# Two strips' exponents by one matmul of twelve rows, and the mask added second and only on the diagonal blocks

## The chip, the cores and the metric

The kernel runs on one core of one Trainium2 chip. The time is the device time of one execution in microseconds. The kernel before took 896.44 us (median of three runs, 891.09 to 898.82). TensorE is the matmul engine (PE in the profile, its weight loads PEld), VectorE is DVE, ScalarE is ACT, GpSimd is POOL, SyncE is SP and issues the DMAs here.

## What is computed

The input is x of 32 sequences, 256 tokens, 128 features, in f32. Four layers follow one another, each `x = x + layer(layernorm(x))`: a gated delta-rule attention, a feed-forward layer, a state-space layer, the same feed-forward layer. The change is in the state-space layer only:

```
zxbcdt = h @ W_in                                 # z 256, xBC 512, dt 4 columns
xBC = silu(causal_conv(xBC, 4 taps)); x, B, C = split(xBC)   # 4 heads of 64; state 128
dt = softplus(dt + dt_bias);  A = -exp(A_log)
# state-space scan over the whole sequence, per head:
#   y[i] = sum over j <= i of  (C[i].B[j]) * exp(S[i] - S[j]) * dt[j] * x[j]
#   S = running sum of dt*A
y = (y + x * D) * silu(z)
y = y * rsqrt(mean(y*y) + eps) * norm_w;  out = y @ W_out
```

The reference writes the scan in chunks of 32 with a carried state; the kernel computes the same as one masked product over all 256 tokens of a sequence. For that it needs, per sequence and head, a matrix of exp(S[i] - S[j]) for j <= i and zero elsewhere. With the source token j on 128 partitions it is cut in two strips: source tokens 0 to 127 against all 256 targets, and source tokens 128 to 255 against targets 128 to 255, 256 + 128 = 384 columns (the name TRI).

## The kernel before, in words

A group is four tiles of 128 tokens, which is two sequences (called batches in the code). There are 16 groups. The state-space part is a software pipeline of 18 halves, `space_half`: half h convolves and projects group b = h, makes exponents, products and scores of group e = h - 1, and outputs of group f = h - 2; up to half 9 it also normalises and transposes the x of a later group (x, turn), and projects dt of a later group (d). Each engine has its own instruction stream, written out by hand in this order, with semaphores between them; there is no planner. TensorE's order in a half is `space_half` from L1779: gate projection L1738, exponents of head 0 of sequence 1 (`log_decay(e, 0, 1)`), head outputs L1761 of group f in two parts with a convolution L1734 between them, transposes L1769 and L1476, exponents (0, 0), L1734, dt projection L1718 (d), exponents (1, 1), products of B and C L1775, exponents (1, 0) and (2, 1) in a row, the sum of squares L1832, gate projection L1738, exponents (2, 0), L1769, L1734, exponents (3, 1) and (3, 0) in a row, the output projection L1853, L1734.

The exponents S[i] - S[j] are themselves made on TensorE, by `log_decay`, in f16 with f32 accumulation. S is split into three f16 pieces (`split_sums`, PIECES = 3; the last is scaled and weighted by TINY). For each group of a quad (four groups, j of them at partitions 32 j) six partitions hold, in turn, piece rows and constant rows: `from_rows` has the pieces of S on even partitions and the weights on odd ones, `to_rows` the negative weights on even and the pieces on odd. A product of the two over the six rows gives S[i] - S[j]. The mask `never16` has -30000 where the target lies before the source (in the two diagonal 128 x 128 blocks) and zero in the block between. One exponent group in `log_decay` is three matmuls into one PSUM bank: the mask times an f16 identity over all 384 columns (L1747), six rows over 256 columns for the first strip (L1748), six rows over 128 columns for the second (L1750). Then ScalarE takes the exponential of the 384 columns (L897), GpSimd multiplies by the products of C and B (L644), and L1761 multiplies by x. A half has eight groups, and there are 16 halves with them: 128 groups.

The pieces reach `from_rows` and `to_rows` through DRAM. Once per quad, SyncE writes `pieces` to `pieces_dram` (L511), waits for it, and issues for each of the quad's four groups two DMAs, one into `from_rows` (L517) and one into `to_rows` (L518), each of three runs of 4096 bytes. There are two sides of the rows, for even and odd quads. The constants of each side are first filled by GpSimd in `set_rows` (L637, two casts of 2048 columns a side): side 0 in the preparation before the first half, side 1 behind half 0. VectorE makes `ident16` and `never16` once (L1213 to L1216). TensorE waits for a group's rows by `pieces_in` at L1784.

VectorE adds an output to x in `add_residual` (L1224), and L1761 of the next half waits for that. ScalarE normalises (L741), makes the first tap (L876); VectorE makes the other three (L1352).

Of the kernel before, what the change touches and what calls it, by code (L numbers as in the profile page):

```python
# [5 lines left out]
BATCH, SEQ, DIM = 32, 256, 128  # L6
# [6 lines left out]
P = 128  # L13
TILES = BATCH * SEQ // P
GROUP_TILES = 4
# [16 lines left out]
PIECES = 3  # L32
TINY = 2.0 ** -12
# [17 lines left out]
def constants():  # L51
# [21 lines left out]
def build(nc, x_in, Wq, bq, Wk, bk, Wv, bv, Wa, ba, Wb, bb, Wg, bg, Wo, bo,  # L73
# [7 lines left out]
    with ctx:  # L81
# [19 lines left out]
        tab = sb("tab", [P, (4 + len(LEVELS)) * P + 2 + LEAF * LEAF])  # L101
# [5 lines left out]
        from_side, to_side = (tab[:, after_keep + P + k:after_keep + P + k + 1] for k in range(2))  # L107
        two_eye = tab[0:GROUP_TILES * LEAVES, after_keep + P + 2:]
# [100 lines left out]
        from_rows, to_rows = ([flat_ff[u][:, k * 2 * GROUP:(k + 1) * 2 * GROUP].bitcast(f16) for u in U] for k in range(2))  # L209
# [4 lines left out]
        ident16, never16 = sb("ident16", [P, P], f16), sb("never16", [P, TRI], f16)  # L214
# [209 lines left out]
        def _(sp):  # L424
# [80 lines left out]
            for q in range(GROUPS // QUAD):  # L505
                side = q % 2
                sp.wait_ge(split_step, SPLITS * (q + 1))
                if q >= 2:
                    for j in range(QUAD):
                        sp.wait_ge(pieces_in[side][j], 16 * 2 * (q // 2))  # L510
                sp.dma_start(pieces_dram[side].rearrange("m r c -> r m c"), pieces[:, :, :]).then_inc(pieces_out, 16)  # L511
                sp.wait_ge(pieces_out, 16 * (q + 1))
                sp.wait_ge(rows_set, 2 * min(q + 1, 2))
# [16 lines left out]
        def _(pool):  # L530
# [438 lines left out]
        def _(dve):  # L969
# [244 lines left out]
            for strip_at in (0, SEQ):  # L1214
                nc.vector.tensor_copy(never16[:, strip_at:strip_at + P], never).then_inc(prep_done, 1)
            nc.vector.tensor_copy(never16[:, P:SEQ], eye_zero[:, P:2 * P]).then_inc(prep_done, 1)  # L1216
# [695 lines left out]
```

## Time and profile before

| | |
|---|---|
| median of three runs | 896.44 us |
| the three runs | 896.44, 891.09, 898.82 us |
| the profiled execution | 890.48 us |
| its span, first to last instruction | 888.6 us |
| PE busy | 783.3 us (88%) |
| DVE busy | 627.1 us (71%) |
| POOL busy | 562.5 us (63%) |
| ACT busy | 537.4 us (60%) |
| mean granted TensorE clock | 0.944 of full |

The span is that of the same execution as the 890.48. The first feed-forward layer starts at about 352 us (the attention before it) and ends at about 436 us, the preparation of the state-space part lies between 436 and 485 us, its first exponent group at 485.5 us, its last at 777.5 us, and the second feed-forward layer starts at about 798 us. A row of a timeline joins instructions of one line that follow one another. A matmul's recorded duration reaches on past the start of the next matmul, so durations of neighbours overlap.

### The profile page before, as it was taken

What the parts mean: (1) busy time and instruction counts of PE and PEld (TensorE: products, weight loads), DVE (VectorE), ACT (ScalarE), POOL (GpSimd) and SP (SyncE); (2) the same over time, 40 slices, a digit from 0 to 9 for tenths busy, and PEclk for the clock granted to TensorE, in tenths of its full rate; (3) what the DMA queues carried; (4) which work ended last, traced back from release to release, by engine and by line L of the source; (5) the groups of instructions that cost most, each with busy time, mean ns of one, the idle gap of its engine ahead of it and who ended that gap; (6) DMA issues with size and microseconds to landing.
All of it is one profiled execution on the core that took longest, in us unless ns stands there. A gap on an engine that the chain in (4) does not pass through costs nothing. (4 is left out here: it accounts for less than half of the span.)

```text
span 888.6 us, 16307 instructions
## 1 busy us (share of the span) xinstructions
PE 783.3 (88%) x5274; PEld 557.7 (63%) x5274; DVE 627.1 (71%) x1740; ACT 537.4 (60%) x1036; POOL 562.5 (63%) x899
## 2 busy tenths in 40 slices
PE   1379999999999895999748999999999999959997
PEld 1268888888888773666534456555555555546665
DVE  1356778777778643888665868988787776537885
ACT  2224443344344324989645878888888787728885
POOL 0266566666766611887632488769778866757785
PEclk9859999999999899999956999999999999979999
DMA  7411211111121100000000000000000000000112
GB/s 215 110 27 31 51 28 28 41 42 27 28 54 28 28 14 1 1 1 0 2 0 7 0 2 7 3 1 1 8 1 1 8 1 1 1 0 25 47 48 72
DMA packets 57740, 22.07 MB, mean 25 GB/s; under 512 B 20960, under 2 KB 57312, under 8 KB 57664
## 3 DMA queue, kind: packets, MB, share of 16 engines
q1 hardware_dynamic: 57664, 21.13, 9.2%
q8 instruction: 38, 0.62, 0.3%
q14 instruction: 38, 0.31, 0.1%
HBM read 11.49 MB, written 9.63 MB: 24 GB/s over the span
## 5 line engine op out<-in xcount | busy, mean ns | idle before, releaser
L1352 DVE SCALAR_TENSOR_TENSOR arena<-bank,convw_sb,arena 128x510 f32<-128x510 f32 (+2 forms) x192 | 142.6, 745 | 37.3 <-ACT arena L876 32.5
L644 POOL TENSOR_TENSOR arena<-arena 128x768 f32<-128x768 f32 x64 | 115.0, 1817 | 12.9 <-ACT arena L903 12.9
L621 POOL TENSOR_TENSOR arena<-ff,arena 128x512 f16<-128x512 f32 x64 | 73.7, 1161 | 23.1 <-ACT arena L844 21.0
L556 POOL TENSOR_TENSOR leaf_tmp<-leafV 32x14 f32<-32x14 f32 (+6 forms) x224 | 56.2, 251 | 33.0 <-DMA leafV<-LT_dram 17.8
L741 ACT ACTIVATE xn<-x_all,shift,rstd 128x128 f32<-128x128 f32 x136 | 55.6, 480 | 33.3 <-DVE shift L988 33.2
L1734 PE MATMUL bank<-xnT,win_sb 128*128 128x512 f32 x128 | 72.5, 651 | 3.2 <-DVE arena L1352 3.2
L839 ACT ACTIVATE ff<-bank 128x512 f32<-128x512 f32 x96 | 56.3, 586 | 30.9 <-PE bank L1645 30.7
L540 POOL TENSOR_TENSOR var_eps<-mv,eps_cols 128x4 f32<-128x4 f32 x34 | 7.6, 223 | 105.0 <-DVE mv L981 86.5
L748 ACT ACTIVATE ff<-bank 128x256 f32<-128x256 f32 (+2 forms) x80 | 34.0, 425 | 66.0 <-PE bank L1489 37.5
L560 POOL TENSOR_TENSOR leafV<-leafV,leaf_tmp 32x14 f32<-32x14 f32 (+6 forms) x224 | 62.6, 279 | 17.5
L897 ACT ACTIVATE arena<-bank 128x384 f32<-128x384 f32 x128 | 60.1, 491 | 21.9 <-PE bank L1750 21.7
L1178 DVE SCALAR_TENSOR_TENSOR ff<-bank,ff 128x512 f32<-128x512 f32 x96 | 64.7, 684 | 10.0 <-ACT ff L839 9.4
L733 ACT ACTIVATE xnT<-bank 128x512 f32<-128x512 f32 x34 | 20.2, 596 | 77.8 <-PE bank L1476 77.8
L650 POOL TENSOR_TENSOR arena<-arena 128x512 f32<-128x512 f32 x32 | 40.3, 1272 | 38.2 <-DVE arena L1359 37.9
L1015 DVE SCALAR_TENSOR_TENSOR arena<-bank,arena 128x256 f32<-128x256 f32 (+1 forms) x128 | 44.6, 411 | 25.0 <-PE bank L1561 16.0
L876 ACT ACTIVATE arena<-bank,convb_sb,convw_sb 128x512 f32<-128x512 f32 x64 | 49.9, 779 | 12.0 <-PE bank L1734 12.0
L1761 PE MATMUL bank<-arena 128*64 128x256 f32 (+1 forms) x512 | 48.5, 332 | 1.7 <-DVE x_all L1224 1.2
L1476 PE MATMUL bank<-tab,xn 128*128 128x128 f32 x136 | 24.6, 311 | 27.8 <-issue 16.5
L1761 PEld LDWEIGHTS bank<-arena 128*64 128x64 f32 x512 | 31.8, 136 | 24.3 <-issue 13.7
L1644 PE MATMUL bank<-xh,gate 128*128 128x512 f16 x96 | 37.7, 393 | 8.6 <-DVE xl L1163 7.9
L1747 PE MATMUL bank<-never,ident 128*128 128x384 f16 x128 | 42.4, 331 | 0.6 <-ACT arena L897 0.6
L844 ACT ACTIVATE arena<-ff 128x512 f16<-128x512 f32 x64 | 39.8, 622 | 3.4 <-DVE ff L1178 3.4
(202 smaller groups left out, 2260.6 us busy)
## 6 DMA issues: line engine op xcount, KB each, us to landing
LT_dram<-arena SPq DMA_DIRECT2D x16, 256.0 KB, 2.4
ff<-R_dram SPq DMA_DIRECT2D x16, 256.0 KB, 2.9
out<-x_all SPq DMA_DIRECT2D x8, 512.0 KB, 3.2
x_all<-in_L_attn_a_x SPq DMA_DIRECT2D x7, 512.0 KB, 7.0
tab<-in_tables SPq DMA_DIRECT2D x1, 513.0 KB, 5.2
x_all<-in_L_attn_a_x SPq DMA_DIRECT2D x2, 256.0 KB, 3.1
R_dram<-tab SPq DMA_DIRECT2D x2, 256.0 KB, 2.7
leafV<-LT_dram SPq DMA_DIRECT2D x16, 32.0 KB, 2.6
```

The lines of the kernel that those rows point to most:

```text
L556: nc.gpsimd.tensor_tensor(prod, V[:, s:s + 1, s + 1:LEAF].broadcast_to([leaf_rows, s, below]), V[:, 0:s, s:s + 1].broadcast_to([leaf_rows, ...
L560: nc.gpsimd.tensor_tensor(V[:, 0:s, s + 1:LEAF], V[:, 0:s, s + 1:LEAF], prod, ALU.subtract).then_inc(leaf_step, 1)
L621: nc.gpsimd.tensor_tensor(of_block(hl[u], j), hidT[u][:, j, :], of_block(hh[u], j), ALU.subtract).then_inc(hl_done[u], 1)
L644: nc.gpsimd.tensor_tensor(score[h], cb[g % 2], hgam[h], ALU.mult).then_inc(score_done, 1)
L741: last = nc.scalar.activation(xn[u][:, cols(t)], x_all[:, n % GROUPS * GROUP + t * P:n % GROUPS * GROUP + (t + 1) * P], ACT.Identity, scal ...
L839: nc.scalar.activation(silu_g[u][:, j, :], bank[u][(1, 3, 1)[j]][:, :], ACT.Silu, scale=DEQUANT).then_inc(silu_done[u], 1)
L876: nc.scalar.activation(xbc[r][b % 2], conv_bank[r % 2][:, :], ACT.Identity, scale=convw_sb[:, r, TAPS - 1:TAPS], bias=convb_sb[:, r:r + 1] ...
L897: nc.scalar.activation(hgam[h][:, batch * TRI:(batch + 1) * TRI], step_bank[batch][:, 0:TRI], ACT.Exp).then_inc(hgam_done, 1)
L1178: nc.vector.scalar_tensor_tensor(hidT[u][:, j, :], bank[u][(2, 0, 2)[j]][:, :], DEQUANT, silu_g[u][:, j, :], ALU.mult, ALU.mult).then_inc( ...
L1352: nc.vector.scalar_tensor_tensor(acc_of[:, :, s:SEQ], src_of[:, :, 0:SEQ - s], convw_sb[:, r, TAPS - 1 - s:TAPS - s], acc_of[:, :, s:SEQ], ...
L1734: mm(conv_bank[r % 2][:, :], win_sb[:, INNER + r * P:INNER + (r + 1) * P], xnT[b % XNT_SETS][:, :], start=True, stop=True).then_inc(conv_m ...
L1761: last = mm(y_bank[r][k * HEAD_DIM:(k + 1) * HEAD_DIM, batch * SEQ + c * P:(batch + 1) * SEQ], x_of[:, 2 * batch + c, h * HEAD_DIM:(h + 1) ...
```

## The change

`log_decay` has two matmuls instead of three. The first has twelve rows: six for each strip. Both strips' pieces stand on twelve partitions of `from_rows`, which now has 128 columns for a head instead of 256: the first strip's source tokens on rows 0 to 5, the second's on rows 6 to 11. `to_rows` has 384 columns for a head instead of 256; a strip's six rows are zero in the other strip's columns. One matmul of 384 columns then gives both strips and opens the accumulation. The second matmul adds the mask, times the identity, and only in columns 0 to 127 and 256 to 383 of the bank; `never16` has 256 columns instead of 384.

Each of the quad's DMAs is cut in two, one a strip, with runs of 256 or 512 bytes, so four for a group (PIECE_DMAS) instead of two. `set_rows` has three copies instead of two for a side, of 1024, 2048 and 1024 columns. The tables have one more column. VectorE makes `never16` with two casts instead of three.

```diff
-    piece, side = (r % 32) // 2, r % 2
-    weight = np.where(piece < PIECES - 1, 1.0, np.where(piece == PIECES - 1, TINY, 0.0))
+    of_strip, side = (r % 32) // 2, r % 2
+    strip_at, piece = of_strip // PIECES, of_strip % PIECES
+    weight = np.where(strip_at > 1, 0.0, np.where(piece < PIECES - 1, 1.0, TINY))
     parts.append((weight * (side == 1)).astype(np.float32))
-    parts.append((-weight * (side == 0)).astype(np.float32))
+    for k in range(2):
+        parts.append((-weight * (side == 0) * (strip_at == k)).astype(np.float32))
...
                 for j in range(QUAD):
-                    src = pieces_dram[side][:, j * BATCHES * HEADS:(j + 1) * BATCHES * HEADS, :].rearrange("m r c -> m (r c)")
-                    sp.dma_start(from_rows[side][32 * j:32 * j + 2 * PIECES:2, :], src).then_inc(pieces_in[side][j], 16)
-                    sp.dma_start(to_rows[side][32 * j + 1:32 * j + 1 + 2 * PIECES:2, :], src).then_inc(pieces_in[side][j], 16)
+                    src = pieces_dram[side][:, j * BATCHES * HEADS:(j + 1) * BATCHES * HEADS, :]
+                    of_quad = slice(32 * j, 32 * (j + 1))
+                    for k in range(2):
+                        at = 2 * PIECES * k
+                        froms = from_rows[side][of_quad, :].rearrange("p (r c) -> p r c", c=P)[at:at + 2 * PIECES:2]
+                        tos = to_rows[side][of_quad, :].rearrange("p (r c) -> p r c", c=TRI)[at + 1:at + 1 + 2 * PIECES:2, :, k * SEQ:k * P + SEQ]
+                        sp.dma_start(froms, src[:, :, k * P:(k + 1) * P]).then_inc(pieces_in[side][j], 16)
+                        sp.dma_start(tos, src[:, :, k * P:SEQ]).then_inc(pieces_in[side][j], 16)
...
             def set_rows(side):
-                for dst, weight in ((from_rows[side], from_side), (to_rows[side], to_side)):
-                    nc.gpsimd.tensor_copy(dst, weight.broadcast_to([P, 4 * GROUP])).then_inc(rows_set, 1)
+                nc.gpsimd.tensor_copy(from_rows[side], from_side.broadcast_to([P, 2 * GROUP])).then_inc(rows_set, 1)
+                of_head = to_rows[side].rearrange("p (r c) -> p r c", c=TRI)
+                for k, strip_cols in enumerate((slice(0, SEQ), slice(SEQ, TRI))):
+                    nc.gpsimd.tensor_copy(of_head[:, :, strip_cols],
+                                          to_side[k].unsqueeze(1).broadcast_to([P, BATCHES * HEADS, SEQ - k * P])).then_inc(rows_set, 1)
...
-                rows = slice(32 * j, 32 * j + 2 * PIECES)
+                rows = slice(32 * j, 32 * j + 4 * PIECES)
                 to = step_bank[batch]
-                a = (batch * HEADS + h) * SEQ
+                at = batch * HEADS + h
                 pe.wait_ge(hgam_done, past(decay_at(e, h, batch) - BATCHES))
-                mm(to[:, 0:TRI], ident16[:, :], never16[:, :], start=True, stop=False)
-                mm(to[:, 0:SEQ], from_rows[side][rows, a:a + P], to_rows[side][rows, a:a + SEQ],
-                   start=False, stop=False)
-                mm(to[:, SEQ:TRI], from_rows[side][rows, a + P:a + SEQ], to_rows[side][rows, a + P:a + SEQ],
-                   start=False, stop=True).then_inc(E_mm, 1)
+                mm(to[:, 0:TRI], from_rows[side][rows, at * P:(at + 1) * P], to_rows[side][rows, at * TRI:(at + 1) * TRI],
+                   start=True, stop=False)
+                mm(to[:, 0:TRI].rearrange("p (s c) -> p s c", c=P)[:, 0:3:2, :], ident16[:, :],
+                   never16[:, :].rearrange("p (s c) -> p s c", c=P), start=False, stop=True).then_inc(E_mm, 1)
```

## Rows read from the trace of the kernel before

**Rows 1.** The page, part 1: busy time of each engine, its share of the span, instructions.
```profile
PE 783.3 (88%) x5274; PEld 557.7 (63%) x5274; DVE 627.1 (71%) x1740; ACT 537.4 (60%) x1036; POOL 562.5 (63%) x899
```

**Rows 2.** Sums by window: stretch, length, each engine's busy time (instructions), clock, DMA.
```profile
500.00:520.00 20.00, 18.66 (x103) 10.71 (x103) 15.45 (x38) 15.27 (x28) 12.24 (x10) 0.91 0.00 1
540.00:560.00 20.00, 20.00 (x127) 12.21 (x127) 15.77 (x36) 16.96 (x32) 17.85 (x18) 1.00 0.03 9
```

**Rows 3.** TensorE's timeline, 561 to 582 us: start, duration, instruction, tiles, form, count.
```profile
561.35 1.02 PE L1734 MATMUL bank<-xnT,win_sb 128*128 128x512 f32 x2
562.22 1.02 PE L1738 MATMUL bank<-xnT,win_sb 128*128 128x512 f32 x2
563.07 0.33 PE L1747 MATMUL bank<-never,ident 128*128 128x384 f16 x1
563.33 0.28 PE L1748 MATMUL bank<-ff 6*128 6x256 f16 x1
563.45 0.21 PE L1750 MATMUL bank<-ff 6*128 6x128 f16 x1
563.60 1.52 PE L1761 MATMUL bank<-arena 128*64 128x256 f32 x16
565.05 1.12 PE L1734 MATMUL bank<-xnT,win_sb 128*128 128x512 f32 x2
566.10 1.52 PE L1761 MATMUL bank<-arena 128*64 128x256 f32 x16
567.55 0.66 PE L1769 MATMUL bank<-tab,arena 128*128 128x128 f32 x4
568.04 0.60 PE L1476 MATMUL bank<-tab,xn 128*128 128x128 f32 x4
568.48 0.33 PE L1747 MATMUL bank<-never,ident 128*128 128x384 f16 x1
...
569.00 1.12 PE L1734 MATMUL bank<-xnT,win_sb 128*128 128x512 f32 x2
569.97 0.95 PE L1718 MATMUL bank<-win_sb,xnT 128*128 128x4 f32 x8
...
573.76 1.05 PE L1832 MATMUL bank<-ones_col,arena 128*128 128x1 f32 x8
...
578.55 2.05 PE L1853 MATMUL bank<-wout_sb,arena 128*128 128x128 f32 x16
580.44 1.02 PE L1734 MATMUL bank<-xnT,win_sb 128*128 128x512 f32 x2
...
582.16 0.33 PE L1747 MATMUL bank<-never,ident 128*128 128x384 f16 x1
```

**Rows 4.** TensorE's timeline in the second feed-forward layer.
```profile
847.38 1.11 PE L1670 MATMUL bank<-downT,ff 128*128 128x128 f32 x8
848.33 0.38 PE L1644 MATMUL bank<-xh,gate 128*128 128x512 f16 x1
```

**Rows 5.** TensorE's timeline in a half with a quad's sums; in brackets its idle time.
```profile
591.56 1.54 PE L1775 MATMUL bank<-arena 128*128 128x256 f32 x8 [0.43 <-issue]
```

**Rows 6.** By source line: nanoseconds least, median, most; first and last start; forms.
```profile
L1216 DVE CAST never<-tab x1: 222/222/222, 437.0 to 437.0; 128x128 f16<-128x128 f32 x1
L637 POOL CAST ff<-tab x4: 1883/1889/1896, 445.5 to 475.7; 128x2048 f16<-128x2048 f32 x4
```

**Rows 7.** SyncE's timeline: the first DMA issue of quad 0, and two of quad 1.
```profile
468.11 0.76 SPq L517 DMA_DIRECT2D ff<-pieces_dram  x1
...
549.92 0.65 SPq L517 DMA_DIRECT2D ff<-pieces_dram  x1
550.61 0.65 SPq L518 DMA_DIRECT2D ff<-pieces_dram  x1
```

**Rows 8.** ScalarE's and VectorE's timelines in the half of rows 3, two rows.
```profile
576.25 0.49 ACT L897 ACTIVATE arena<-bank 128x384 f32<-128x384 f32 x1 [1.37 <-PE bank L1750]
...
581.20 1.12 DVE L1224 SCALAR_TENSOR_TENSOR x_all<-bank,arena,x_all 128x128 f32<-128x128 f32 x4
```

More of the change, by code:

```diff
@@ L32 @@
 PIECES = 3
+PIECE_DMAS, ROW_SETS = 4, 3
 TINY = 2.0 ** -12
@@ L100, in build @@
         x_all = sb("x_all", [P, TILES * DIM])
-        tab = sb("tab", [P, (4 + len(LEVELS)) * P + 2 + LEAF * LEAF])
+        tab = sb("tab", [P, (4 + len(LEVELS)) * P + 3 + LEAF * LEAF])
         ident, eye_zero = tab[:, 0:P], tab[:, 0:2 * P]
@@ L106, in build @@
         never = tab[:, after_keep:after_keep + P]
-        from_side, to_side = (tab[:, after_keep + P + k:after_keep + P + k + 1] for k in range(2))
-        two_eye = tab[0:GROUP_TILES * LEAVES, after_keep + P + 2:]
+        from_side, *to_side = (tab[:, after_keep + P + k:after_keep + P + k + 1] for k in range(3))
+        two_eye = tab[0:GROUP_TILES * LEAVES, after_keep + P + 3:]
         half_neg = sb("half_neg", [P, STREAMS * GROUP_TILES])
@@ L208, in build @@
         flat_ff = [ff[u][:, :, :].rearrange("p k c -> p (k c)") for u in U]
-        from_rows, to_rows = ([flat_ff[u][:, k * 2 * GROUP:(k + 1) * 2 * GROUP].bitcast(f16) for u in U] for k in range(2))
+        from_rows, to_rows = ([flat_ff[u][:, a:b].bitcast(f16) for u in U] for a, b in ((0, GROUP), (GROUP, 4 * GROUP)))
         row_tmp = [flat_ff[u][0:QROWS, 4 * GROUP + k * SEQ:4 * GROUP + (k + 1) * SEQ] for u in U for k in range(4)]
@@ L213, in build @@
         pieces = sb("pieces", [QROWS, PIECES, SEQ], f16)
-        ident16, never16 = sb("ident16", [P, P], f16), sb("never16", [P, TRI], f16)
+        ident16, never16 = sb("ident16", [P, P], f16), sb("never16", [P, SEQ], f16)
         pieces_dram = [nc.dram_tensor(f"pieces_dram{k}", [PIECES, QROWS, SEQ], f16).ap() for k in range(2)]
@@ L509, in _ @@
                     for j in range(QUAD):
-                        sp.wait_ge(pieces_in[side][j], 16 * 2 * (q // 2))
+                        sp.wait_ge(pieces_in[side][j], 16 * PIECE_DMAS * (q // 2))
                 sp.dma_start(pieces_dram[side].rearrange("m r c -> r m c"), pieces[:, :, :]).then_inc(pieces_out, 16)
                 sp.wait_ge(pieces_out, 16 * (q + 1))
-                sp.wait_ge(rows_set, 2 * min(q + 1, 2))
+                sp.wait_ge(rows_set, ROW_SETS * min(q + 1, 2))
                 sp.wait_ge(E_mm, past(2 * HEADS * QUAD * (q - 1) - 1))
                 for j in range(QUAD):
-                    src = pieces_dram[side][:, j * BATCHES * HEADS:(j + 1) * BATCHES * HEADS, :].rearrange("m r c -> m (r c)")
-                    sp.dma_start(from_rows[side][32 * j:32 * j + 2 * PIECES:2, :], src).then_inc(pieces_in[side][j], 16)
-                    sp.dma_start(to_rows[side][32 * j + 1:32 * j + 1 + 2 * PIECES:2, :], src).then_inc(pieces_in[side][j], 16)
+                    src = pieces_dram[side][:, j * BATCHES * HEADS:(j + 1) * BATCHES * HEADS, :]
[6 more added lines that the diff above has]
+                        sp.dma_start(tos, src[:, :, k * P:SEQ]).then_inc(pieces_in[side][j], 16)
             out_tok = out.rearrange("b (c p) d -> p (b c) d", p=P)
@@ L1213, in _ @@
             nc.vector.tensor_copy(ident16[:, :], ident).then_inc(prep_done, 1)
-            for strip_at in (0, SEQ):
-                nc.vector.tensor_copy(never16[:, strip_at:strip_at + P], never).then_inc(prep_done, 1)
-            nc.vector.tensor_copy(never16[:, P:SEQ], eye_zero[:, P:2 * P]).then_inc(prep_done, 1)
+            for k in range(2):
+                nc.vector.tensor_copy(never16[:, cols(k)], never).then_inc(prep_done, 1)
             def add_residual(e):
@@ L1709, in _ @@
                 pe.wait_ge(x_done, upto(2 * PAIRS, u))
-            pe.wait_ge(prep_done, INNER_BLOCKS + 5)
+            pe.wait_ge(prep_done, INNER_BLOCKS + 4)
             def of_token(d):
@@ L1783, in space_half @@
                     gate(e, 0)
-                    pe.wait_ge(pieces_in[e // QUAD % 2][e % QUAD], 16 * 2 * (e // QUAD // 2 + 1))
+                    pe.wait_ge(pieces_in[e // QUAD % 2][e % QUAD], 16 * PIECE_DMAS * (e // QUAD // 2 + 1))
                     log_decay(e, 0, 1)
```

## The prediction

> **What bounds the kernel now.** I read the page first. TensorE is busy for 88% of the span, more than any other engine [rows 1], but ends of matmuls are modelled there, so this alone proves nothing. Next came the sums by window. In an ordinary stretch of the state-space part, 540 to 560 us, TensorE is busy for all 20.00 of 20 us at the full clock (1.00, the 2.4 GHz level), while VectorE, ScalarE and GpSimd leave 4.2, 3.0 and 2.2 us [rows 2]. Early in the part (500 to 520 us) the granted clock is 0.91 and TensorE is 1.3 us short of busy.
>
> The timeline settles it. Rows there overlap, since a matmul's record runs on after the next has begun; the honest price of an instruction is the distance to the next start. From one head-0 exponent group (563.07) to that of the next half (582.16) is 19.09 us without one idle gap in the rows [rows 3]. So every TensorE nanosecond taken out of a half shortens it, until another engine's chain of about that length takes over.
>
> **One exponent group before.** L1747, L1748 and L1750 start at 563.07, 563.33 and 563.45, and the next work at 563.60 [rows 3]: 0.53 us. Of that:
> - L1747 moves 384 columns, 0.16 us at 2.4 GHz, yet L1748 starts 0.26 later: 0.10 more.
> - L1748 moves 256 columns (0.11) in 0.12: nearly no loss.
> - L1750 moves 128 columns (0.05) and the next work starts 0.15 later: 0.09 more.
>
> The two losses stand where a matmul of 6 rows meets one of 128 rows. I call that a switch and price it at 0.10 going in and 0.09 coming out. The Trainium skill (TensorEngine Tiling, Tiling Modes, Key Properties) says that changing the tiling mode drains TensorE; the trace agrees, with 0.10 and 0.09 us.
>
> There is a third loss, one instruction later. The pair L1734 takes 0.87 to the next start behind ordinary 128-row work (561.35), but 0.97 right behind the group (569.00). L1718 and L1832, eight small f32 matmuls each, last 0.95 and 1.05; the longer is the one behind the group. L1853 takes 1.89 for 16 f32 matmuls of 128 columns (578.55 to 580.44); the four L1476 take 0.44, so 0.11 each, and 16 of them 1.78: 0.11 over. The transposes L1769 last 0.66 behind a switch, L1476 0.60 behind them: 0.05 to 0.06 [rows 3]. I read this as the second f32 weight load, which is not hidden when the work right after a switch is f32.
>
> **The change, part by part.**
>
> *The group itself.* New order: a 12-row matmul of 384 columns, then the identity over 256 columns. Switch in 0.10, 384 columns 0.16, weights 0.01, switch out 0.09, 256 columns 0.12 (L1748's own): 0.48 against 0.52, so 0.04 less; eight groups a half give 0.34. Two of the eight follow another group directly, where L1747 took 0.01 longer: 0.02 more saved.
>
> *The follower.* Now the f16 identity comes first after the switch and the f32 follower's weights load behind its 256 columns. Nearest row: in the feed-forward part eight L1670 (f32) stand behind f16 matmuls of only 128 columns, and take 0.95 to the next start, where 8 x 0.11 are 0.88: 0.06 of a load still shows behind 0.06 us of cover [rows 4]. So a load needs about 0.11 us of cover, and the identity gives 0.12. I take the loss as gone: L1734, L1775, L1832 and L1853 0.10 each (L1775 taken as the others), L1769 0.05: 0.45 a half.
>
> *One new switch.* Head outputs L1761 use 64 columns of the array, a third layout. Before, the group left its 6-row layout straight for it, in 0.15 with one switch. Now the identity stands between: one switch more. L1734 to L1761 is such a one: 1.05 (565.05 to 566.10) against the 0.97 of the same pair without it [rows 3], 0.08 to 0.09. Minus 0.09 a half.
>
> A half saves 0.34 + 0.02 + 0.45 - 0.09 = 0.72. Fifteen of the 16 halves with exponent groups have all followers: 10.8. In three of them (once per later quad) TensorE waits 0.43 before the products for VectorE's scan [rows 5], and what group (1,1) and its follower save is waited away: -0.15 each, -0.45. For the last half, which has no next group's projections to fill TensorE, I choose 0.1 less. The first has no head outputs and lies where TensorE is short of busy; I choose 0.5 for it instead of 0.7. Sum: 10.8 - 0.45 - 0.1 + 0.5 = 10.75.
>
> *Entry from f32.* No row shows f32 followed by a 6- or 12-row matmul; six of eight entries are such. Bounds: 0.10 (f16 to 6 rows) and 0.08 (f32 to 64 columns); I take 0.10, nearest in layout. Nothing excludes more.
>
> *Preparation.* VectorE has one cast fewer, of 0.22 us by itself [rows 6] and about half of that behind its like: -0.1. GpSimd fills the same 4096 columns a side, at 1889 ns for 2048 [rows 6], in three instructions instead of two; side 0 is filled from 445.5 on, by 449.3, and the first DMA into it starts at 468.11 [rows 7], so nothing is late. The upper bound is 0.1 a side if a third start costs; the lower is a gain: VectorE's small operations that stall beside these casts might slip in at the new boundary up to 0.9 us earlier. I take 0.
>
> *The DMAs.* SyncE issues 16 instead of 8 a quad, 0.65 each [rows 7]. The first four of quad 1 are issued by 549.92 + 4 x 0.65 = 552.5 instead of 551.2 for the first two, and are needed at 563.07 [rows 3]. Each later set has a whole half (19 us) for 2.6 us of issue. SyncE has no other DMA queued behind them until the part is over. An issue would have to take 2.5 us, four times its row, to be late. Cost nothing; without this cover it would be 8 x 0.65 = 5.2 us a quad. The new pieces are runs of 256 and 512 bytes. The Trainium skill (DMA: Bandwidth & Descriptors, Specifications) wants 512 bytes or more for full rate; no row here holds 256-byte runs, and it alters no term above.
>
> Total: 10.75 + 0.1, so **10.9 us less**. Against the profiled execution's own 890.48 that is 879.6; against the median 896.44 it is 885.5. The profiled one lies 6 us below the median of the three, 0.6 below the fastest. I say 885.
>
> **What is late next.** ScalarE waits 1.37 us a half for TensorE before the head-2 exponential [rows 8]. From that release its chain (normalise, first tap) feeds VectorE, whose residual ends at 581.20 + 1.12 = 582.32, 0.36 before the head outputs that need it (one group's 0.53 after 582.16). On TensorE this stretch shortens by 0.20 (three groups' 0.13, followers L1769 and L1853 0.15, less the new switch's 0.09), and the group's end tells ScalarE some 0.08 later, since the last matmul is longer: slack 0.08 is left. The whole loop outside TensorE is 19.09 - 1.37 = 17.7 us, below the new 18.4. So TensorE stays the bound, narrowly in this stretch.
>
> **Rivals.**
> 1. *Followers keep their loss.* The Trainium skill (TensorE: Matmul & The Clock Gate, Part 3) says that a weight load overlaps running matmuls only where row groups differ; the identity and the f32 weights use the same rows. As a mechanism here: 0.45 a half stays, and 0.27 is saved, 4.3 us in all: 892. Against it: L1734 behind L1853, same rows, loses nothing; for it: L1670's 0.06. Chance 0.13.
> 2. *Another chain takes over.* The 0.08 of slack is negative instead, or VectorE's taps come late, and a third of the gain turns into waits on L1224 or L1352: about 7 us saved, 889. Chance 0.15.
> 3. *Slower: the entry from f32.* Place: in front of six groups a half. If it costs 0.22 instead of 0.10, the 0.72 is eaten; beyond that the kernel is slower, and at 0.32 by about 0.6 x 16 = 10 us: 906. For it: such entries never occurred. Against it: leaving and entering in other pairs always costs 0.08 to 0.10. Chance 0.05.
> 4. *The clock.* TensorE's clock was 0.91 from 500 to 520 us [rows 2]; the group now moves 640 columns instead of 768, 384 of them over 12 rows only. Five us more at the lower level would give back 2.5 of TensorE's work: 888 to 890. Chance 0.07.
>
> The forecast has the remaining 0.60.
>
> **How the numbers follow.** The unknown entry, followers and boundaries move the forecast by 2 us either way, and single runs spread over 891.09 to 898.82, so its own range is 880 to 890. Down to 879 it takes in the low runs; up to 892.5 it takes in rivals 1, 2 and 4. About 1% (9 us, 887.5) is what can be told from no change. Of the forecast three quarters lie below it (0.46), and of the others a spread of low runs adds 0.09: faster 0.55. Slower is rival 3 beyond 1%, with an accident: 0.04. The rest, 0.41, is same.
>
> **What would show it.** TensorE's timeline after: 12-row matmul to identity 0.26; identity to a 128-row follower 0.12; L1718's group's 0.95 also for L1832; pair L1734 at 0.87 everywhere behind groups; identity to L1761 0.20; a half at 18.4 us where it is 19.09 now. The forecast falls if 0.97 stays (rival 1), if new waits on L1224 or L1352 stand before TensorE's rows (rival 2), or if f32 to 12 rows takes over 0.15 (rival 3).

## The result and the profile after

The changed kernel takes 886.75 us (median of 20 runs, 882.14 to 896.29) where the kernel before takes 896.40 (median of 20 runs beside them, 888.04 to 900.73). The ratio is 0.9902, 95% interval 0.988 to 0.9924: faster by about 9 us. In a second session the same kernel took 884.75 us (6 runs), ratio 0.9866 (0.9833 to 0.99). The forecast was 885 us, with a range of 879 to 892.5, and faster. The first profiled execution of the changed kernel was its slowest run (896.29 us), so the rows of after come from the second session: 887.27 us, span 885.5 us, granted clock 0.943.

The page, part 1, of the changed kernel: 128 TensorE instructions fewer than in [rows 1], which is one matmul in each of 128 exponent groups.

```profile
PE 780.3 (88%) x5146; PEld 556.0 (63%) x5146; DVE 626.1 (71%) x1739; ACT 537.6 (61%) x1036; POOL 562.6 (64%) x901
```

TensorE's timeline of one half of the changed kernel (start, duration, instruction, tiles, form, count). Lines have moved: L1734 and L1738 are L1744 and L1748, L1748 and L1750 together are L1757 (the twelve rows), the mask L1747 is L1759, L1761 is L1770, L1769 is L1778, L1476 is L1486, L1718 is L1728, L1775 is L1784, L1832 is L1841, L1853 is L1862.

```profile
565.90 0.33 PE L1757 MATMUL bank<-ff 12*128 12x384 f16 x1
566.16 0.28 PE L1759 MATMUL bank<-never,ident 128*128 128x256 f16 x1
566.37 1.52 PE L1770 MATMUL bank<-arena 128*64 128x256 f32 x16
...
570.33 0.66 PE L1778 MATMUL bank<-tab,arena 128*128 128x128 f32 x4
570.82 0.60 PE L1486 MATMUL bank<-tab,xn 128*128 128x128 f32 x4
571.36 0.33 PE L1757 MATMUL bank<-ff 12*128 12x384 f16 x1
571.62 0.28 PE L1759 MATMUL bank<-never,ident 128*128 128x256 f16 x1
571.74 1.02 PE L1744 MATMUL bank<-xnT,win_sb 128*128 128x512 f32 x2
572.60 0.95 PE L1728 MATMUL bank<-win_sb,xnT 128*128 128x4 f32 x8
...
576.21 0.95 PE L1841 MATMUL bank<-ones_col,arena 128*128 128x1 f32 x8
577.02 1.10 PE L1748 MATMUL bank<-xnT,win_sb 128*128 128x512 f32 x2
578.05 0.33 PE L1757 MATMUL bank<-ff 12*128 12x384 f16 x1
...
580.70 1.95 PE L1862 MATMUL bank<-wout_sb,arena 128*128 128x128 f32 x16
...
584.30 0.33 PE L1757 MATMUL bank<-ff 12*128 12x384 f16 x1
```

Read it beside [rows 3]. Head-0 exponent group to head-0 exponent group is 584.30 - 565.90 = 18.40 us, where it was 19.09. The pair L1744 behind a group takes 0.86 to the next start (571.74 to 572.60) where L1734 took 0.97, L1841 lasts 0.95 where L1832 lasted 1.05, L1862 1.95 where L1853 lasted 2.05. Late in the part, where nothing is normalised for later groups any more, a half is 17.11 us where it was 17.84.

Why the follower is shorter can be seen in its weight loads (PEld). First the kernel before: the two loads of the pair L1734 start with its first matmul, at 569.00. Then the changed kernel: the first load of the pair L1744 starts with the identity, at 571.62, and is 0.12 us old when its matmul starts at 571.74.

```profile
568.86 0.21 PE L1750 MATMUL bank<-ff 6*128 6x128 f16 x1
...
569.00 0.30 PEld L1734 LDWEIGHTS bank<-xnT,win_sb 128*128 128x128 f32 x2 [0.16 <-issue]
```

```profile
571.62 0.31 PEld L1744 LDWEIGHTS bank<-xnT,win_sb 128*128 128x128 f32 x2
```

### The profile page after: what moved, and what is told of

Same layout as the page of the kernel before. It is cut to its first block and busy times, and to the rows that moved or that the text cites. A ratio compares the mean times of both kernels' runs of the same rounds, so it can differ in the third digit from the quotient of the medians.

```text
span 894.4 us, 16084 instructions
## 1 busy us (share of the span) xinstructions
PE 787.6 (88%) x5146; PEld 560.4 (63%) x5146; DVE 624.7 (70%) x1739; ACT 537.3 (60%) x1036; POOL 561.3 (63%) x901
## 5 line engine op out<-in xcount | busy, mean ns | idle before, releaser
L1362 DVE SCALAR_TENSOR_TENSOR arena<-bank,convw_sb,arena 128x510 f32<-128x510 f32 (+2 forms) x192 | 142.5, 745 | 34.7 <-ACT arena L887 30.1
L1744 PE MATMUL bank<-xnT,win_sb 128*128 128x512 f32 x128 | 72.4, 651 | 1.7 <-DVE arena L1362 1.7
L887 ACT ACTIVATE arena<-bank,convb_sb,convw_sb 128x512 f32<-128x512 f32 x64 | 50.0, 782 | 11.6 <-PE bank L1744 11.6
L1770 PE MATMUL bank<-arena 128*64 128x256 f32 (+1 forms) x512 | 48.5, 332 | 3.5 <-DVE x_all L1234 2.4
L1770 PEld LDWEIGHTS bank<-arena 128*64 128x64 f32 x512 | 31.9, 136 | 25.6 <-issue 11.7
L1486 PE MATMUL bank<-tab,xn 128*128 128x128 f32 x136 | 24.5, 311 | 26.6 <-issue 16.5
L1757 PEld LDWEIGHTS bank<-ff 12*128 12x128 f16 x128 | 11.7, 91 | 54.5 <-issue 29.0
L1757 PE MATMUL bank<-ff 12*128 12x384 f16 x128 | 43.9, 343 | 0.8 <-ACT arena L908 0.8
```

Source lines behind the costliest of these rows:

```text
L1362: nc.vector.scalar_tensor_tensor(acc_of[:, :, s:SEQ], src_of[:, :, 0:SEQ - s], convw_sb[:, r, TAPS - 1 - s:TAPS - s], acc_of[:, :, s:SEQ], ...
L1744: mm(conv_bank[r % 2][:, :], win_sb[:, INNER + r * P:INNER + (r + 1) * P], xnT[b % XNT_SETS][:, :], start=True, stop=True).then_inc(conv_m ...
L1770: last = mm(y_bank[r][k * HEAD_DIM:(k + 1) * HEAD_DIM, batch * SEQ + c * P:(batch + 1) * SEQ], x_of[:, 2 * batch + c, h * HEAD_DIM:(h + 1) ...
```

## Experiments

Every kernel below ran beside the kernel before on the same chip, and ratios are to that. The theories: **A**, the gain comes from the order and the size of the mask. It stands second, covers the next f32 weights, and moves 256 columns instead of 384; that two matmuls became one is worth little. **B**, the gain comes from issuing one matmul fewer. **C**, what is now late next is ScalarE's order in front of the residual.

**The change repeated.** 

> The changed kernel once more, for a second profile and a fresh ratio beside the others. Theory A (order and columns: the f16 identity comes last, so the f32 follower's weights are covered, and 128 columns fewer are moved): 9 to 10 us under the kernel before, ratio 0.989 to 0.991; halves of 18.40 and 17.11 us at the full clock, with waits of 0.1 to 0.6 us for the residual in front of the head outputs of two to four halves. Theory B (one matmul of twelve rows instead of two of six is what pays): the same time.

Measured: 884.75 us, ratio 0.9866 (0.9833 to 0.99), 12 us where 9 to 10 were expected; the interval takes in both. Its rows are the ones above.

**The mask first again, over 384 columns, the twelve rows kept.**

```diff
-                mm(to[:, 0:TRI], from_rows[...], to_rows[...], start=True, stop=False)
-                mm(to[...diagonal blocks...], ident16[:, :], never16[...], start=False, stop=True).then_inc(E_mm, 1)
+                mm(to[:, 0:TRI], ident16[:, :], never16[:, :], start=True, stop=False)
+                mm(to[:, 0:TRI], from_rows[...], to_rows[...], start=False, stop=True).then_inc(E_mm, 1)
```

> Twelve rows kept (two matmuls a group), but the mask comes first again and over all 384 columns. Theory A: 384 columns 0.16, switch in 0.10, 384 columns 0.17, switch out 0.09, so 0.52 us a group as before the change, and the follower's loss of 0.10 is back; the new switch in front of the 64-column head outputs is gone: no gain at all, ratio 0.998 to 1.002, a half 19.1 us. Theory B: the merged matmul keeps most of the gain, ratio 0.990 to 0.993.

Measured: 897.52 us, ratio 0.9984 (0.9949 to 1.0018). Merging alone gives nothing. TensorE's timeline of this kernel:

```profile
742.28 0.33 PE L1759 MATMUL bank<-ff 12*128 12x384 f16 x1
742.54 1.57 PE L1784 MATMUL bank<-arena 128*128 128x256 f32 x8
...
744.74 0.33 PE L1759 MATMUL bank<-ff 12*128 12x384 f16 x1
745.00 1.05 PE L1841 MATMUL bank<-ones_col,arena 128*128 128x1 f32 x8
```

The followers are back at their long durations (1.57 and 1.05, against 1.47 and 0.95 of the changed kernel's late halves), and halves are 19.07 and 17.83 us, those of the kernel before.

**The mask second, but over 384 columns.**

```diff
-                mm(to[...diagonal blocks...], ident16[:, :], never16[...], start=False, stop=True).then_inc(E_mm, 1)
+                mm(to[:, 0:TRI], ident16[:, :], never16[:, :], start=False, stop=True).then_inc(E_mm, 1)
```

> The changed kernel with the mask second but over all 384 columns instead of 256. Theory A: 128 columns more cost 0.053 us a group, 8 x 16 groups, 6.8 us over the changed kernel less what is waited away at the residual (about 1 us): ratio to the kernel before 0.995 to 0.998, identity to a 128-row follower 0.17 instead of 0.12 us. If instead the columns were free and the order all that counts: the changed kernel's own ratio, 0.990.

Measured: 891.78 us, ratio 0.9939 (0.9906 to 0.9973). Its timeline:

```profile
741.43 0.34 PE L1760 MATMUL bank<-never,ident 128*128 128x384 f16 x1
741.61 0.95 PE L1841 MATMUL bank<-ones_col,arena 128*128 128x1 f32 x8
```

The follower is short (0.95), and the identity takes 0.17 to the next start where the narrow one takes 0.12. The ratio is a little below the 0.995 to 0.998 expected, but its interval reaches into that. Halves are 18.77 and 17.52 us. So of the 0.72 us that a late half gained (17.84 to 17.11), 0.31 is the order and 0.41 the narrower mask (17.52 to 17.11).

**Everything but the merging: the kernel before, its three matmuls, its DMAs and fills, with the mask second and narrow.**

```diff
-                mm(to[:, 0:TRI], ident16[:, :], never16[:, :], start=True, stop=False)
-                mm(to[:, 0:SEQ], from_rows[...], to_rows[...], start=False, stop=False)
-                mm(to[:, SEQ:TRI], from_rows[...], to_rows[...], start=False, stop=True).then_inc(E_mm, 1)
+                mm(to[:, 0:SEQ], from_rows[...], to_rows[...], start=True, stop=False)
+                mm(to[:, SEQ:TRI], from_rows[...], to_rows[...], start=False, stop=False)
+                mm(to[...diagonal blocks...], ident16[:, :], never16[...], start=False, stop=True).then_inc(E_mm, 1)
```

> The kernel before with its two matmuls of six rows (and its rows, DMAs and fills), but these first and the mask second, in the diagonal blocks only: three matmuls a group. Theory A: 256 and 128 columns are as many as the 384 of the merged one and one weight load more is hidden, so 0.48 to 0.50 us a group and all the followers' gain: ratio 0.989 to 0.992, within 0.002 of the changed kernel. Theory B: no merging, no gain: 0.998 to 1.002. Between the changed kernel and this one also lie the DMAs (32 instead of 64) and GpSimd's fills; by theory A these are worth under 1 us.

Measured: 887.97 us, ratio 0.9889 (0.985 to 0.9928). Its timeline:

```profile
743.65 0.28 PE L1746 MATMUL bank<-ff 6*128 6x256 f16 x1
743.77 0.21 PE L1748 MATMUL bank<-ff 6*128 6x128 f16 x1
743.91 0.28 PE L1750 MATMUL bank<-never,ident 128*128 128x256 f16 x1
744.13 0.28 PE L1746 MATMUL bank<-ff 6*128 6x256 f16 x1
```

Two matmuls of six rows take 743.91 - 743.65 = 0.26 to the identity, and the one of twelve rows takes 0.26 too. Halves are 18.42 and 17.13 us, 0.02 from those of the change. Theory B falls: the twelve rows, with their doubled DMAs, third copy and new table column, bought nothing that can be measured.

**Where cover ends.** The next three kernels cut the mask itself. Unmasked blocks would overflow the exponential, so all three scale its input by 1e-06, and the first of them, with the full mask, is their control.

```diff
-                                     ACT.Exp).then_inc(hgam_done, 1)
+                                     ACT.Exp, scale=1e-06).then_inc(hgam_done, 1)
```

> Control for the next two: the changed kernel, but ScalarE's exponential multiplies its input by 1e-06, so that all decays are close to 1 (the output is another). No instruction is added or removed. Every theory: halves of 18.40 us in the ordinary stretch and 17.11 late in the part, ratio to the kernel before 0.988 to 0.991, as the changed kernel itself. If the data alone moved the clock or the time, it would show here.

Measured: 886.15 us, ratio 0.9894 (0.9865 to 0.9923), halves of 18.40 and 17.11 us. The other data change nothing that can be told.

The mask over one diagonal block:

```diff
-                mm(to[...diagonal blocks...], ident16[:, :], never16[...], start=False, stop=True).then_inc(E_mm, 1)
+                mm(to[:, 0:P], ident16[:, :], never16[:, 0:P], start=False, stop=True).then_inc(E_mm, 1)
```

> As soft_decay, and the identity moves 128 columns instead of 256 (one diagonal block is left unmasked). Theory A (the identity is the cover behind which the first f32 weights of the next work load; a load needs about 0.11 us of cover): the identity's pitch falls from 0.12 to 0.06 us, and the four f32 followers get 0.05 of their 0.10 back as a loss: pair at 0.91 to 0.92 instead of 0.86, eight small matmuls at 1.00. A half saves 8 x 0.06 less 4 x 0.05 = 0.28: late halves 16.83 instead of 17.11. Rival B (followers lost their 0.10 to the six-row matmul in front of them, and cover has no part in it): followers stay at 0.86 and 0.95, late halves 17.11 - 0.48 = 16.63. Rival C (all or nothing: cover shorter than a load hides nothing): followers lose all 0.10: 17.11 - 0.48 + 0.45 = 17.08. In the ordinary stretch (18.40) the residual's slack of 0.07 caps the gain of either theory at about 0.1 to 0.3.

No mask at all:

```diff
-                   start=True, stop=False)
-                mm(to[...diagonal blocks...], ident16[:, :], never16[...], start=False, stop=True).then_inc(E_mm, 1)
+                   start=True, stop=True).then_inc(E_mm, 1)
```

> As soft_decay, and the exponent group is its twelve-row matmul alone (no block is masked). Theory A: the twelve-row matmul to the next work stays at 0.26, the identity's 0.12 goes from eight groups, the switch in front of the head outputs goes with it (0.09), but four f32 followers lose 0.10 and the transposes 0.05 again: 0.96 + 0.09 - 0.45 = 0.60 a half, late halves 16.51; pair at 0.97, eight small at 1.05, sixteen wide at 2.05. Rival B: nothing is lost behind the twelve-row matmul, 1.05 a half, late halves 16.06. In the ordinary stretch the residual becomes the bound: TensorE waits on VectorE before the head outputs in nearly every half, and halves are 17.8 to 18.1 instead of 17.3 to 17.8. Whole kernel: 0.979 to 0.983 of the time before under A, 0.971 to 0.976 under B.

Measured with one block: 889.17 us, ratio 0.9928 (0.9895 to 0.9962). Its timeline, late in the part:

```profile
739.51 0.23 PE L1759 MATMUL bank<-never,ident 128*128 128x128 f16 x1
739.58 1.00 PE L1840 MATMUL bank<-ones_col,arena 128*128 128x1 f32 x8
...
743.90 0.23 PE L1759 MATMUL bank<-never,ident 128*128 128x128 f16 x1
743.97 2.00 PE L1861 MATMUL bank<-wout_sb,arena 128*128 128x128 f32 x16
```

And with none: 889.45 us, ratio 0.9928 (0.9906 to 0.9951). Its timeline; in brackets, idle time of the engine before the row and what ended it:

```profile
737.67 0.33 PE L1757 MATMUL bank<-ff 12*128 12x384 f16 x1
737.93 0.66 PE L1776 MATMUL bank<-tab,arena 128*128 128x128 f32 x4
...
739.80 2.05 PE L1860 MATMUL bank<-wout_sb,arena 128*128 128x128 f32 x16
...
743.51 0.33 PE L1757 MATMUL bank<-ff 12*128 12x384 f16 x1
744.28 1.52 PE L1768 MATMUL bank<-arena 128*64 128x256 f32 x16 [0.45 <-DVE x_all L1234]
```

The same sixteen matmuls last 1.95, 2.00 and 2.05 us behind 256, 128 and no columns of identity, and the eight small ones 0.95, 1.00 and (in another row of that timeline) 1.05. For the followers that is theory A to the hundredth: a narrower cover gives most of its saving back. Late halves are 16.90 us with one block (16.83 expected) and 16.8 with none, of which 0.45 is the new wait in the last row. Without it they would be 16.3, where theory A said 16.51 and rival B 16.06. The 0.2 is a term that I had left out: two groups in a row now have no switch between them, and start 0.17 us apart (739.38 and 739.55) instead of the 0.26 that a group takes in front of other work; there are two such pairs a half.

But neither kernel is faster than its control, and here my expectation of 0.979 to 0.983 failed. Part of the reason is in TensorE's waits (view of waits, 480 to 780 us: engine, line, waited for, us in total, times, longest). First the changed kernel, then the one without a mask:

```profile
PE bank L1770 <- DVE x_all L1234: 2.4, 3, 1.4
```

```profile
PE bank L1768 <- DVE x_all L1234: 9.1, 12, 1.2
```

The head outputs waited for the residual in 12 halves, and ordinary halves came out between 17.4 and 18.6 us. From the first to the last exponent group this profile takes 285.8 us and its control's takes 287.8, so little of what TensorE saved is left. The other part is the clock. This profile is that of the fastest of the kernel's twelve runs (882.84 us, granted clock 0.947). The median clock of the twelve is 0.930, against 0.939 in the six of the control, and among the twelve each 0.01 of clock goes with about 3.3 us, so some 3 us of the median (889.45 against 886.15) are that. The kernel with one block shows the same (median clock 0.933 in seven runs). Why their clock was lower the runs don't show.

**ScalarE's order.** The slack at the residual is 0.07 us in the changed kernel. Its chain begins with ScalarE's normalise, with the first tap of the convolution behind it; I swapped the two.

```diff
-                if x is not None:
-                    normalise_of(*x)
                 if b is not None:
                     first_tap(b, 2)
+                if x is not None:
+                    normalise_of(*x)
```

> The changed kernel with one swap on ScalarE: in a half, the first tap of block 2 before the four normalisations (1.64 us) instead of behind them, so that VectorE's taps of block 2 and the residual behind them come up to 1.6 us earlier. Theory C (what is lost of the gain in three halves is waiting for the residual, 0.58, 0.15 and 0.46 us): these waits are gone, ordinary halves stay 18.40, and the kernel is 1.2 us faster than the changed one, ratio 0.985 to 0.989 if that one's is 0.9866 to 0.990. Rival (VectorE, not ScalarE, holds the residual back, since its queue has no idle time in those halves): the waits stay, no gain.

Measured: 897.86 us, ratio 1.0029 (1.0001 to 1.0056), where theory C said 0.985 to 0.989 and its rival no gain: the whole gain of the change is gone. ScalarE's waits in the changed kernel and in this one, same view and stretch:

```profile
ACT arena L887 <- PE bank L1744: 7.8, 15, 1.6
```

```profile
ACT arena L887 <- PE bank L1744: 23.2, 22, 6.6
```

And ScalarE's timeline of this kernel in one half:

```profile
579.81 0.49 ACT L908 ACTIVATE arena<-bank 128x384 f32<-128x384 f32 x1 [0.59 <-PE bank L1759]
581.11 0.78 ACT L887 ACTIVATE arena<-bank,convb_sb,convw_sb 128x512 f32<-128x512 f32 x1 [0.81 <-PE bank L1744]
581.78 1.64 ACT L752 ACTIVATE xn<-x_all,shift,rstd 128x128 f32<-128x128 f32 x4
583.32 0.85 ACT L908 ACTIVATE arena<-bank 128x384 f32<-128x384 f32 x2
```

The tap's input is a projection that TensorE makes behind the exponent group just taken (L1744 at 580.04). So ScalarE stands 0.81 us at the head of its queue, and the normalise and the two exponentials behind it are late by that; the normalise used to run in exactly that time. The old order was the one that filled the wait. VectorE pays for it: its waits for this tap (L1362 for L887) are 45.9 us in 33 times, against 28.7 in 23 in the changed kernel.

Theory C falls, and its rival had the mechanism right. Two of the three waits for the residual stayed as they were (0.57 and 0.14 us, at 626.62 and 645.23), and three new ones came (0.41, 0.15 and 0.19). VectorE holds the residual back there: in the changed kernel it has no idle time over 0.04 us from 612.06 until the residual ends at 623.41.

That is not yet the whole loss. From the first to the last exponent group this profile takes 297.3 us, the changed kernel's 288.4. Of the 8.8 us, 6.6 lie in three halves (21.58, 20.28 and 21.63 us instead of 19.64, 17.80 and 19.42) in which the granted clock is lower too: 0.91, 0.92 and 0.86 at 580 to 600, 640 to 660 and 680 to 700 us, where the changed kernel has 1.00, 1.00 and 0.91. What the order costs by itself and what the clock adds, this run doesn't separate.

**Two groups' twelve-row matmuls together, then their two masks** (where two groups follow one another; fewer switches between layouts).

```diff
-                    log_decay(e, 1, 0)
-                    log_decay(e, 2, 1)
+                    log_decay(e, (1, 0), (2, 1))
...
-                    log_decay(e, 3, 1)
-                    log_decay(e, 3, 0)
+                    log_decay(e, (3, 1), (3, 0))
```

> The changed kernel, but where two exponent groups follow one another, (1,0) with (2,1) and (3,1) with (3,0), both twelve-row matmuls come first and then both masks: one switch in and out for two groups. Theory A: 0.20 us less a pair, 0.40 a half, 6.4 us in 16 halves; but in the halves that normalise the residual has only 0.07 us of slack, and of the 0.40 the 0.20 of pair (3,1), (3,0) stands in front of it, so 10 halves give only 0.27: 5 us, ratio to the kernel before 0.981 to 0.985. Late halves 16.7 instead of 17.11. If a switch's cost were in truth a cost of each weight load, nothing would be gained: 0.987 to 0.990.

Measured: 886.66 us, ratio 0.9916 (0.9879 to 0.9953), where 0.981 to 0.985 was expected. Its profiled execution had a granted clock of 0.95 even in ordinary stretches, so its pitches are not compared. With ScalarE's order swapped as well:

> Both edits: paired masks, and the first tap in front of the normalisations. Theories A and C together: the whole 0.40 a half, 6.4 us, and 1.2 us of residual waits: 7.6 us under the changed kernel, ratio to the kernel before 0.978 to 0.982, ordinary halves 18.0, late ones 16.7. If ScalarE's order is not what holds the residual: as paired alone.

Measured: 895.04 us, ratio 0.9991 (0.9963 to 1.0019), where 0.978 to 0.982 was expected; the swap spoils this one too. Late halves of this one, at full clock, are 16.79 us against 17.11: pairing does free 0.32 us of TensorE a half (0.40 expected). In the median of the paired kernel alone none of it is seen, as in the kernels with less mask.

**A second profile of the kernel before**, for the clock.

> The kernel before, unchanged, for a second profile. Of the clock: in the three profiles with the mask last and in the diagonal blocks only (two of the changed kernel, one with six rows) the clock stays at its lower level for 10.2 us from about 515 to 532 us, in the first profile of the kernel before and with the mask first for 3.4 us. If that belongs to the change, it is 3.4 us here; if to chance, it may be either. Halves of 19.09 and 17.85 in any case.

Measured: 895.31 us. Sums by window (stretch, length, busy time of PE, PEld, DVE, ACT, POOL with instructions, granted clock, DMA share, GB/s) from 490 to 530 us, for the first profile of the kernel before, then this second one, then the changed kernel:

```profile
490.00:530.00 40.00, 37.61 (x211) 21.81 (x212) 30.09 (x70) 31.57 (x57) 26.77 (x23) 0.91 0.00 1
```

```profile
490.00:530.00 40.00, 37.40 (x183) 20.63 (x183) 27.75 (x70) 29.73 (x54) 23.30 (x19) 0.83 0.00 1
```

```profile
490.00:530.00 40.00, 36.90 (x166) 20.06 (x166) 30.51 (x72) 30.41 (x54) 23.32 (x19) 0.83 0.00 1
```

Over these 40 us two profiles of one and the same kernel differ by 0.08. But the expectation was about the low stretch that follows 510 us, and there the second profile is like the first. The stretch from 505 to 535 us, in the second profile of the kernel before and then in the changed kernel:

```profile
505.00:535.00 30.00, 29.13 (x175) 16.66 (x174) 22.51 (x52) 24.26 (x42) 21.33 (x19) 0.94 0.00 1
```

```profile
505.00:535.00 30.00, 28.39 (x153) 16.10 (x149) 21.52 (x47) 22.15 (x39) 19.22 (x19) 0.83 0.00 1
```

A clock of 0.94 over 30 us is 3.4 us at the lower level, 0.83 is 10.2. All four profiles with a mask of 384 columns have 0.94 there (two of the kernel before, the mask first, the mask wide). Of the nine with a narrower mask or none, eight are lower: 0.77 and 0.83 in the changed kernel, 0.83 with six rows, in the control, with one block and with both of the last edits, 0.89 without a mask, 0.74 with paired masks alone. Only the swapped order on ScalarE by itself has 0.94. The mask first, the mask wide, six rows and the second profile of the changed kernel all come from one chip. So the longer low stretch goes with the change, as the first reading of the expectation said, though not in every kernel that has it. What makes it longer stays open.

The spans of the single profiles are 888.6, 893.5 and 885.5 us: the changed kernel's is 3.1 us below the one and 8.0 below the other.

## Why the prediction was right

The group, the followers and the half came out as worked out. That the whole kernel came so near to the forecast is in part luck: two rivals took nearly half of the sum back in the traces, and the medians differ by more than the traces account for. The paragraphs on the sum and on the clock have the numbers.

**The group.** Said: switch in 0.10, out 0.09, twelve rows to identity 0.26, identity to a 128-row follower 0.12. Measured between 530 and 765 us, in the starts of the trace in nanoseconds: 0.263 to 0.264 for nearly all of 103 groups, and 0.119 to 0.120 for nearly all of the 62 with such a follower. Right.

**The followers.** Said: the identity hides the first f32 weights, 0.45 a half. Shown three ways: they are short with the mask second, long with it first, and half way with half the cover. The weight loads above show it directly; it is the first of the follower's loads that moves ahead, and not the second, as one sentence of the prediction has it. I had read the 0.11 us that a load needs from [rows 4], and the half cover bears it out: behind 0.06 us of identity 0.05 is lost. This was also rival 1, and it is out. The Trainium skill (TensorE: Matmul & The Clock Gate, Part 3) says in its list of what overlaps that a weight load overlaps running matmuls only where the row groups differ. The trace disagrees here: f32 weights of 128 rows start to load at 571.62, together with a 128-row identity, at no cost that shows.

**The new switch.** Said: 0.20 from the identity to the head outputs. Measured 0.21. Right.

**The entry from f32.** The one price that no row of before gave, taken as 0.10. The second of a pair L1748 takes 0.429 us to an f32 follower and 0.525 to the twelve-row matmul: 0.096. Rival 3, the slower side, had its place and nothing in it.

**Preparation and DMAs.** Said: cost nothing, issues of 0.65 us each. Two of SyncE's rows in the changed kernel:

```profile
554.08 0.70 SPq L525 DMA_DIRECT2D ff<-pieces_dram  x1
...
565.00 0.68 SPq L526 DMA_DIRECT2D ff<-pieces_dram  x1
```

These are the first and the last of quad 1's sixteen: 0.73 us apart, 11.6 us in all. The first group's four are issued by 557, its exponents start at 565.90, and no wait of TensorE for a DMA stands in the view of waits. Nothing was late.

**The half.** Said: 0.72 less, 18.4. Measured: 18.40 and 17.11, which is 0.69 and 0.73 less.

**What is late next.** Said: slack of 0.08 at the residual. Rows of the changed kernel, ScalarE and VectorE:

```profile
578.64 0.49 ACT L908 ACTIVATE arena<-bank 128x384 f32<-128x384 f32 x1 [0.93 <-PE bank L1759]
579.03 1.64 ACT L752 ACTIVATE xn<-x_all,shift,rstd 128x128 f32<-128x128 f32 x4
...
583.59 1.12 DVE L1234 SCALAR_TENSOR_TENSOR x_all<-bank,arena,x_all 128x128 f32<-128x128 f32 x4
```

The residual ends at 584.71 and the head outputs start at 584.77 (the group of 584.30, two matmuls later): 0.06 to 0.07. The size was right. The reasoning beside it was not: I gave the loop outside TensorE 17.7 us, "below the new 18.4", as if that were the distance to the next bound. The loops that bind run through TensorE, and there are two.

The first goes from the head outputs to the head-2 exponential by TensorE, 12.65 us before (563.60 to 576.25, [rows 3, 8]) and 12.27 now (566.37 to 578.64), and from there to the residual's end by ScalarE's tap and VectorE, 6.07 us in both. That is 18.72 of 19.09 before and 18.34 of 18.40 now. The second goes from the head outputs to the dt projection by TensorE, 7.22 us (566.37 to 573.59), and from there by VectorE alone, which has no idle time over 0.04 us until 584.71: 11.12 us, 18.34 too. VectorE's last taps, first in the kernel before, then in the changed one, where the wait for ScalarE is gone:

```profile
578.97 2.31 DVE L1352 SCALAR_TENSOR_TENSOR arena<-bank,convw_sb,arena 128x510 f32<-128x510 f32 x3 [0.63 <-ACT arena L876]
```

```profile
581.36 2.31 DVE L1362 SCALAR_TENSOR_TENSOR arena<-bank,convw_sb,arena 128x510 f32<-128x510 f32 x3
```

In such a half only 0.06 us more can be gained from TensorE behind the dt projection. Without the mask the second loop is what decides. VectorE is released there by

```profile
570.78 0.17 DVE L1241 TENSOR_TENSOR dt_z<-bank,dtb_row 128x16 f32<-128x16 f32 x1 [0.48 <-PE bank L1728]
```

and then has no idle time until the residual ends at 581.67. From the head outputs at 563.59 that is 7.19 + 10.89 = 18.08 us, of a half of 18.14 (563.59 to 581.73). This is also why an earlier tap on ScalarE could not bring the residual forward.

**The sum.** Said: 10.9 us. The ratio gives 896.4 x 0.0098 = 8.8 (6.8 to 10.8), the two medians 9.65, the second session 12.0 (9 to 15). All of these lie near the forecast, but the traces don't show the sum at work. From the first exponent group to the end of the program the two profiles of the kernel before take 403.1 and 407.0 us, the two of the changed kernel 400.2 and 397.6: 6 us less on average, not 10.8. Where the medians' other 3 to 6 us lie, the profiles don't show.

Half by half, the second profile of the changed kernel against the first of the kernel before, 14 halves from the group at 503.68 on: eight save 0.68 to 0.74 each, and the one with a quad's dt transposes, at 584, saves 0.59. Those are the halves that the sum described. In the four from 622 to 697 it failed: they save 0.05, 0.48, 0.06 and -1.57. In the first three of them TensorE waits for the residual, as in this one:

```profile
623.46 1.52 PE L1770 MATMUL bank<-arena 128*64 128x256 f32 x16 [0.57 <-DVE x_all L1234]
```

With the other two (0.15 and 0.46, at 642.08 and 660.19) that is 1.19 us. In the fourth it waits for ScalarE and GpSimd (0.28 at 686.58, 0.12 at 687.73). This is rival 2, and the sum had put it at nothing; only the first of the four follows a quad's running sums on VectorE (612.06 to 614.35). The sum charged the quads 0.45 for the wait before the products [rows 5], and missed these. The first half is 2.74 us longer instead of 0.7 shorter, and 1.6 of the fourth's loss is no wait either; both are the clock.

**The clock.** Rival 4 said: five us more at the lower level, 2.5 given back. In the traces this came about, beside the forecast and not in its place. The half that begins at 503.68 us, with the clock of 0.83 around it, takes 25.41 us (24.96 in the other profile of the changed kernel), where that half of the kernel before takes 22.67 and 22.14, of the mask first 22.20 and the mask wide 22.34. That is 6.8 us more at the lower level, and about 3.4 given back. A second low stretch lies at 680 to 700 us (0.91 in both profiles of the changed kernel, 1.00 in both of the kernel before): that half takes 19.42 us, and 17.79 in the control with the scaled exponential, which has the same instructions and no such stretch. This one may be chance, since the second profile of the kernel before has one like it at 580 to 600 us (0.91, a half of 21.78 instead of 20.23). Over whole runs no difference can be told: the mean granted clock is 0.938 in 20 runs of the changed kernel and 0.941 in six more, against 0.940 in 23 runs of the kernel before.

## What to carry to other kernels

Where small f16 matmuls stand between f32 ones, put the one with the follower's layout last: behind it the first f32 weights load unseen, and behind a matmul of few rows they do not (0.10 us each time here, 0.05 for the transposes). Undo each part of a change by itself: here the part with most of the code, twelve rows in one matmul, was worth nothing that can be measured, and the order and the size of the mask were worth all. For what is late next, follow every loop through all the engines that it uses, an engine's own queue too, and compare its whole length with the half; the slack of one link does not say how much more can be taken out of another. And before a gain is read from one pair of profiles, compare the same stretch and its clock in all of them.

## What the runs showed of the hardware

- A change between a layout of few rows and one of 128 costs 0.09 to 0.10 us each way, and the same whether six or twelve rows and whether f16 or f32 stands in front (0.096 from f32).
- Behind an f16 matmul of 128 rows the first weight load of an f32 follower starts with that matmul (571.62), 0.12 us ahead of its own; behind one of six rows it starts with its own matmul (569.00).
- The cost of the uncovered load is graded, not all or nothing: 0, 0.05 and 0.10 us behind 256, 128 and 0 columns of f16 identity.
- Two matmuls of six rows back to back (256 and 128 columns, 0.26 us to the identity) take what one of twelve rows and 384 columns takes.
- DMA issues from SyncE with three partition rows each take 0.68 us and follow one another every 0.73, against 0.65 for the longer runs before [rows 7].
- The same 30 us of a program (505 to 535) were granted 0.94 of the clock in four profiles of four with a mask of 384 columns, and 0.74 to 0.89 in eight of nine with a narrower one or none. A low stretch of 3.4 us costs a half about 1.6 us.
